# Second stage of a cross-attention and mixture block: logits of the slot pass stored in DRAM and turned on TensorE for the combine

## The reference

```python
x = x + _L1_ffn_ref(_layernorm(x, axis=-1), L1_ffn_phi, L1_ffn_W, L1_ffn_b)
...
logits = jnp.einsum('bmd,dnp->bmnp', x, phi)
dispatch = jax.nn.softmax(logits, axis=0)
...
combine = jax.nn.softmax(logits.reshape(bsz, m, n * p), axis=-1).reshape(bsz, m, n, p)
slots = jnp.einsum('bmd,bmnp->bnpd', x, dispatch)
y = jnp.einsum('bnpd,nde->bnpe', slots, W) + b[None, :, None, :]
out = jnp.einsum('bnpd,bmnp->bmd', y, combine)
```

## Time and profile before

| what | us |
|---|---|
| median of 3 runs | 6867.51 |
| lowest and highest | 6865.7, 6872.63 |
| the profiled execution | 6864.03 |
| its span | 6862.2 |
| slot pass, first logits to first combine matmul | 4671.4 to 5906.9 |
| combine, first to last matmul | 5906.9 to 6856.7 |

### The profile page before, as it was taken

The page is one execution under the profiler, slowest core; times in us unless marked ns, Lnnn a source line. Parts: engine busy times, 40 slices in busy tenths (PEclk is TensorE's granted clock), DMA queues, the critical chain, the costliest instruction groups (busy, mean ns, idle before and its releaser), DMA issues. The chain is left out here.

```text
span 6862.2 us, 93027 instructions
## 1 busy us (share of the span) xinstructions
PE 6307.0 (92%) x35933; PEld 3091.1 (45%) x35933; DVE 3514.3 (51%) x6804; ACT 3263.7 (48%) x6001; POOL 2408.1 (35%) x2689
## 2 busy tenths in 40 slices
PE   3799999999999999999999999966999999999999
PEld 1223333333333333333333333226888888666666
DVE  3565665665656656656656566516666666000000
ACT  1366666666666666666666666522222222111111
POOL 4226436346355264363463552342222222000000
PEclk9799999999999999999999999968999999999999
DMA  2442332432432423314324324003444444311110
GB/s 64 77 76 57 67 76 56 73 69 63 76 71 55 84 57 66 78 55 73 69 63 76 70 53 75 6 16 135 157 167 154 158 162 163 121 56 56 49 56 31
DMA packets 364938, 546.09 MB, mean 80 GB/s; under 512 B 59824, under 2 KB 281984, under 8 KB 364240
## 3 DMA queue, kind: packets, MB, share of 16 engines
q1 hardware_dynamic: 321232, 498.18, 30.0%
q10 hardware_dynamic: 43264, 41.95, 1.8%
HBM read 387.94 MB, written 151.28 MB: 79 GB/s over the span
## 5 line engine op out<-in xcount | busy, mean ns | idle before, releaser
L1193 DVE TENSOR_REDUCE mx<-psum 128x1 f32<-128x401 f32 x4096 | 2212.9, 570 | 1615.7 <-PE psum L767 1606.6
L1038 ACT ACTIVATE probs<-psum 128x512 f32<-128x512 f32 (+1 forms) x3328 | 1910.6, 599 | 910.4 <-PE psum L789 907.3
L767 PE MATMUL psum<-kst,qst 96*128 96x401 bf16 x4096 | 1356.6, 343 | 192.5 <-DVE mx L1193 149.6
L789 PE MATMUL psum<-qst,kst 99*128 99x512 bf16 (+1 forms) x3328 | 1286.0, 387 | 49.9 <-ACT probs L1038 44.8
L800 PE MATMUL psum<-probs,vaug 128*17 128x512 f32 x6656 | 886.8, 605 | 0.0
L789 PEld LDWEIGHTS psum<-qst,kst 99*128 99x128 bf16 (+1 forms) x3328 | 328.8, 99 | 1178.5 <-ACT probs L1038 748.9
L767 PEld LDWEIGHTS psum<-kst,qst 96*128 96x128 bf16 x4096 | 402.7, 98 | 962.8 <-DVE mx L1193 756.3
L1460 POOL TENSOR_TENSOR disp<-disp,rz 128x2048 f32<-128x2048 f32 x64 | 294.7, 4605 | 905.5 <-DVE rz L1679 905.5
L1479 PE MATMUL psum<-phi,xT 128*128 128x128 f32 x4096 | 511.0, 279 | 39.1 <-DMA xT<-xnT_scratch 31.8
L1630 ACT ACTIVATE disp<-psum 128x512 f32<-128x512 f32 x256 | 152.8, 597 | 807.6 <-PE psum L1547 807.6
L1479 PEld LDWEIGHTS psum<-phi,xT 128*128 128x128 f32 x4096 | 479.0, 193 | 86.8 <-issue 79.1
(11 more groups left out here) (197 smaller groups left out, 7556.2 us busy)
## 6 DMA issues: line engine op xcount, KB each, us to landing
xnb<-xn_scratch SPq DMA_DIRECT2D x256, 512.0 KB, 3.6
kst<-k_planes SPq DMA_DIRECT2D x384, 200.1 KB, 8.8
k_planes<-pl SPq DMA_DIRECT2D x96, 384.0 KB, 3.2
y_scratch<-ysb ACTq DMA_DIRECT2D x128, 256.0 KB, 3.3
disp<-y_scratch SPq DMA_DIRECT2D x16, 2048.0 KB, 9.2
vaug<-v_scratch SPq DMA_DIRECT2D x64, 442.0 KB, 4.6
v_scratch<-vst SPq DMA_DIRECT2D x48, 544.0 KB, 3.1
cin<-in_ctx SPq DMA_DIRECT2D x48, 512.0 KB, 3.8
```

The lines of the kernel that those rows point to most:

```text
L767: mm(to[:, 0:PW], qst[g][0:NP, j, t * P:(t + 1) * P], kst[g][0:NP, j, k0:k0 + PW], start=True, stop=True).then_inc(m_full, 1)
L789: mm(bank[S_BANK[n % 2]][0:m, :], kst[g][0:NR, j, c * P:c * P + m], qst[g][0:NR, j, :], start=True, stop=True).then_inc(s_full, 1)
L1038: fn(probs[0:m, 4 * (k % 2) + j, :], bank[S_BANK[j % 2]][0:m, :], ACT.Exp, scale=float(HD) ** 0.5).then_inc(s_exp, 1)
L1193: v.tensor_reduce(mx[:, n % 2, u // 4, u % 4:u % 4 + 1], bank[M_BANK[r % 2]][:, 0:PW], AX.X, ALU.max).then_inc(m_free, 1)
```

## The change

The combine no longer computes logits. In the slot pass ScalarE's queue stores every tile as soon as it is evacuated (`store_logits`, 1 MB in pieces of 512 bytes, to `logit_scratch`), and VectorE's `front` waits for that store before it overwrites the tile. For the combine SyncE reads a quarter of a batch's logits at a time (`logits_back`, a unit of 1 MB, tokens on partitions), eight units deep, into the memory of `xT`. ScalarE takes the exponentials in place, with the token's maximum as bias and the row sum as a second result (`weights`). TensorE turns four 128x128 blocks into a bank (`transpose_back`), VectorE copies the bank into `exT` (`copy_back`), and `combine` multiplies with 256 columns. The denominators come from the row sums. `ya` and the residuals take the memory of `phi`, `disp` and `xnb`.

```diff
...
+    lg_d = nc.dram_tensor("logit_scratch", (B, QT, P, NS), F32, kind="Internal").ap()
...
+        lgb = xT[:, :, :, :].rearrange("p b k s -> p (b k s)").rearrange("p (u t n) -> p u t n", u=8, t=QT)
...
+        ya = [phi[:, :, :].rearrange("p k n -> p (k n)").rearrange("p (c e) -> p c e", e=D),
+              flat[:, 0:NSL * D].rearrange("p (c e) -> p c e", e=D)]
+        x3 = [xnb[:, i, :, :] for i in range(2)]
+        exT = [flat[:, NSL * D + i * S:NSL * D + (i + 1) * S] for i in range(4)]
...
+
+            def logits_back(u):
+                if u >= 8:
+                    sp.wait_ge(tr_mm, 4 * (u - 7))
+                sp.dma_start(lgb[:, u % 8, :, :], lg_d[u // 4][:, :, QS * (u % 4):QS * (u % 4) + QS].rearrange(
+                    "t p n -> p t n")).then_inc(lg_in[u % 8], 16)
+
+            def values(b, c0, c1):
+                sp.dma_start(ya[b % 2][:, c0:c1, :],
+                             y_d[b].rearrange("(p c) e -> p c e", c=NSL)[:, c0:c1, :]).then_inc(y_in[b % 2], 16)
+
+            def residual(b):
+                sp.dma_start(x3[b % 2], x3_d[b].rearrange("(p t) d -> p t d", t=QT)).then_inc(x3_in[b % 2], 16)
...
+                    if s == NSL - 1 and b == 4:
+                        sp.wait_ge(l_mm, 4 * TILES)
+                        for i in range(2):
+                            sp.wait_ge(lg_stored[i], 16 * (TILES // 2))
+                        logits_back(0)
+                        logits_back(1)
+                    if s == NSL - 1 and b == 10:
+                        for i in range(2):
+                            sp.wait_ge(y_stored[i], 16 * PAIRS * (NSL - 1) // 2)
+                        values(0, 0, NSL - 1)
+
+            for u in range(2, 8):
+                logits_back(u)
+            sp.wait_ge(sl_mm, B * NSL)
+            for i in range(2):
+                residual(i)
...
+            values(0, NSL - 1, NSL)
+            values(1, 0, NSL)
+            for b in range(2, B + 2):
+                for h in range(4):
+                    if 4 * b + h < UNITS:
+                        logits_back(4 * b + h)
+                if b < B:
                     sp.wait_ge(o_mm, NSL * (b - 1))
-                values(b, 0, NSL)
-                if b >= 2:
+                    values(b, 0, NSL)
                     sp.wait_ge(o_stored[b % 2], 16 * (b // 2))
-                residual(b)
+                    residual(b)
...
+            def transpose_back(n):
+                b, e = n // NSL, n % NSL
+                u = 4 * b + e // 4
+                if e % 4 == 0:
+                    pe.wait_ge(c_exp, QT * (u + 1))
+                if n >= 4:
+                    pe.wait_ge(ex_ready, n - 3)
                 for t in range(QT):
-                    last = nc.tensor.transpose(tb[0:3, t * P:(t + 1) * P], ngp[:, t, b, :], identb[:, :])
-                last.then_inc(ng_tr, 1)
-
-            def scores(b, c):
-                n = b * NSL + c
-                if n >= 2:
-                    pe.wait_ge(c_exp, n - 1)
-                o = bank[n % 2]
-                for k in range(2):
-                    mm(o, phi[:, k, c * P:(c + 1) * P], xT[:, b, k, :], start=(k == 0), stop=False)
-                if c == 0:
-                    pe.wait_ge(shift_ready, b + 1)
-                mm(o, ones3[:, :], shift[b % 2], start=False, stop=True).then_inc(c_mm, 1)
-
-            def combine(b, e):
-                n = b * NSL + e
+                    last = nc.tensor.transpose(bank[n % 4][:, t * P:(t + 1) * P],
+                                               lgb[:, u % 8, t, (e % 4) * P:(e % 4 + 1) * P], ident[:, :])
+                last.then_inc(tr_mm, 1)
+
+            def combine(n):
+                b, e = n // NSL, n % NSL
+                pe.wait_ge(ex_ready, n + 1)
                 if e == 0:
-                    pe.wait_ge(y_in[b % 2], 16 * (b // 2 + 1))
-                    if b >= 1:
-                        pe.wait_ge(o_ready, b)
-                pe.wait_ge(c_exp, n + 1)
+                    pe.wait_ge(y_in[b % 2], 16 * (b // 2 + 1 + (b + 1) % 2))
                 for t in range(QT):
-                    last = mm(bank[4 + t][:, 0:D + 1], ex[n % 4][:, t * P:(t + 1) * P], ya[b % 2][:, e, :],
+                    if e == 0 and b >= 1:
+                        pe.wait_ge(o_ready, QT * (b - 1) + t + 1)
+                    last = mm(bank[4 + t][:, 0:D], exT[n % 4][:, t * P:(t + 1) * P], ya[b % 2][:, e, :],
                               start=(e == 0), stop=(e == NSL - 1))
                 last.then_inc(o_mm, 1)
...
+            def store_logits(n):
+                act.wait_ge(l_copied, 4 * n + 4)
+                if n >= 2:
+                    act.wait_ge(lg_stored[n % 2], 16 * (n // 2))
+                act.dma_start(lg_d[:, n % QT, :, (n // QT) * SL:(n // QT + 1) * SL].rearrange("b p n -> p b n"),
+                              disp[:, n % RING, :, :]).then_inc(lg_stored[n % 2], 16)
...
+            def weights(u):
+                b, h = u // 4, u % 4
+                act.wait_ge(lg_in[u % 8], 16 * (u // 8 + 1))
+                if u == 0:
+                    act.wait_ge(nm_ready, 1)
+                if h == 0 and b >= 2:
+                    act.wait_ge(o_den, b - 1)
+                for t in range(QT):
+                    d = lgb[:, u % 8, t, :]
+                    fn(d, d, ACT.Exp, bias=nm[:, t, b:b + 1], accum_out=sums[:, b % 2, t, h:h + 1]).then_inc(c_exp, 1)
...
+                store_logits(n)
...
+                if g == NSL * PAIRS - 2:
+                    weights(0)
...
+                    if g % 2 == 1:
+                        store_logits(n)
...
+            def store_out(b):
+                act.wait_ge(o_ready, QT * (b + 1))
+                act.dma_start(out[b].rearrange("(t p) d -> p t d", p=P), x3[b % 2]).then_inc(o_stored[b % 2], 16)
...
+            for u in range(1, 8):
+                weights(u)
+            for b in range(B):
+                for h in range(4):
+                    if 4 * b + h + 8 < UNITS:
+                        weights(4 * b + h + 8)
+                store_out(b)
...
+                dve.wait_ge(lg_stored[n % 2], 16 * (n // 2 + 1))
...
+                    if n == TILES:
+                        dve.wait_ge(ng_step, TILES)
+                        v.tensor_scalar(nm[:, :, :], negs[:, :, :], -1.0, None, ALU.mult).then_inc(nm_ready, 1)
...
+            def copy_back(n):
+                dve.wait_ge(tr_mm, n + 1)
+                if n >= 4:
+                    dve.wait_ge(o_mm, n - 3)
+                v.tensor_copy(exT[n % 4], bank[n % 4]).then_inc(ex_ready, 1)
+
+            def denominators(b):
+                dve.wait_ge(c_exp, QT * 4 * (b + 1))
+                v.tensor_reduce(den[:, :], sums[:, b % 2, :, :], AX.X, ALU.add).then_inc(o_den, 1)
+                dve.wait_ge(o_den, b + 1)
+                v.reciprocal(rc[:, b % 2, :], den[:, :]).then_inc(o_rc, 1)
+                dve.wait_ge(o_rc, b + 1)
...
             def finish(b):
                 dve.wait_ge(o_mm, NSL * (b + 1))
-                for t in range(QT):
-                    ins = v.reciprocal(rc[:, b % 2, t:t + 1], bank[4 + t][:, D:D + 1])
-                ins.then_inc(o_rc, 1)
-                dve.wait_ge(o_rc, b + 1)
                 dve.wait_ge(x3_in[b % 2], 16 * (b // 2 + 1))
                 for t in range(QT):
-                    ins = v.scalar_tensor_tensor(out=x3[b % 2][:, t, :], in0=bank[4 + t][:, 0:D],
-                                                 scalar=rc[:, b % 2, t:t + 1], in1=x3[b % 2][:, t, :],
-                                                 op0=ALU.mult, op1=ALU.add)
-                ins.then_inc(o_ready, 1)
-
-            shift_rows(0)
-            for b in range(B):
-                if b + 1 < B:
-                    shift_rows(b + 1)
-                finish(b)
+                    v.scalar_tensor_tensor(out=x3[b % 2][:, t, :], in0=bank[4 + t][:, 0:D],
+                                           scalar=rc[:, b % 2, t:t + 1], in1=x3[b % 2][:, t, :],
+                                           op0=ALU.mult, op1=ALU.add).then_inc(o_ready, 1)
...
```

More of the change, by code:

```diff
@@ L1386, in stage_two @@
         ng_step = sem("ng_step")
[L1387 to L1391, removed]
+        nm_ready = sem("nm_ready2")
+        lg_stored = [sem(f"lg_stored{i}") for i in range(2)]
+        lg_in = [sem(f"lg_in{i}") for i in range(8)]
         y_in = [sem(f"y_in{i}") for i in range(2)]
         x3_in = [sem(f"x3_in{i}") for i in range(2)]
-        c_mm = sem("c_mm")
         c_exp = sem("c_exp")
+        tr_mm = sem("tr_mm")
+        ex_ready = sem("ex_ready")
         o_mm = sem("o_mm")
+        o_den = sem("o_den")
         o_rc = sem("o_rc")
@@ L1561, in _ @@
             pe.wait_ge(y_ready, PAIRS * NSL)
[L1562 removed]
+            pe.wait_ge(l_copied, 4 * TILES)
             for n in range(B * NSL + LAG):
[L1564 removed]
                 if n < B * NSL:
[L1566 to L1568 removed]
+                    transpose_back(n)
                 if n >= LAG:
[L1570 removed]
```

(50 more changed lines are left out.)

43 lines of the change are left out of this document (5 added, 38 removed).

## The result

The changed kernel takes **6932.92 us**, the median of five runs (6910.85 to 6939.99), against 6867.51 us (6864.94 to 6872.63, five runs): a ratio of 1.0086, with a 95% interval of 1.0067 to 1.0106. It is slower by 65 us, where 6492 us were forecast. The gain that was forecast and the loss that hides it can both be read from its profile. The profiled execution took 6918.06 us, with a span of 6916.3.

What follows compares the result with a forecast made beforehand. TensorE was taken to bound the slot pass and the combine. The terms -378 - 2 - 8 + 2 + 3 + 6 + 2 = -375 us gave 6489 profiled, 6492 us as median, range 6465 to 6610.

Steps and rivals of the forecast that it cites:

- the likeliest case: Whole kernel: the forecast of 6492 us, given 0.73, with its own range of 6465 to 6530 us.
- The combine tile: Combine: four transposes replace recomputed logits, a tile takes 2.18 us instead of 3.67; 378 us less, plus 2 and 8.
- the rival of doubled ones: Combine: transposes run as full float32 products in two recorded instructions each, 113 us more, 6605 us; chance 0.04.
- What keeps pace in the combine: Combine: VectorE's copy 0.67 us, ScalarE's exponential 0.60, both under 2.18 a tile; transfers need 211 GB/s; nothing counted.
- The store's landing: Slot pass: each 1 MB store in 2048 pieces lands in 6.5 us, with 4.9 and 9.2 as bounds.
- 13.0 us of cover: Slot pass: a landing of up to 6.7 + 6.3 = 13.0 us costs TensorE nothing in steady state.
- the stores also share the DMA engines with the token loads: Slot pass: stores add 1.05 MB to a tile's 2.9 MB; 3 us added, between 0 and 15.
- The rivals of the slow store: Slot pass: landing beyond 13.0 us delays VectorE, middle 6587 us (0.13); from 19.2 us the whole gain goes (0.03).
- The sign of being wrong: Slot pass: steps longer than 9.2 us with VectorE waiting for a DMA of `logit_scratch` would point to the store.
- The first tile: Start of slot pass: VectorE's subtraction waits for the first store, 2 us; 0 if landing in 4.9, 4.3 at 9.2.
- The end of the slot pass: Last slice to first combine product: combine loads queued ahead delay token loads; 6 us later, from 4 earlier to 22 later.
- The clock: End of slot pass: longer TensorE idling may add a second piece at the lower clock level, 2 us.

Runs made afterwards that it cites:

- The kernel with 512 bytes of padding: The changed kernel with the batches of the stored logits 4 MiB + 512 bytes apart instead of 4 MiB: 6507.49 us, ratio 0.9471.
- The kernels with late loads: Combine's first loads moved behind the last token load, against the same layouts with early loads: 8 KB layout 6484.07 us, 512 bytes of padding 6487.32 us.

## Why the prediction was wrong

The kernel with 512 bytes of padding is the changed kernel without the fault. Its median of 6507.5 us is 15 us above the forecast, inside the likeliest case's own range, so its profiled execution (6506.09 us, span 6504.3) serves to measure each term.

- **The combine tile, right.** Forecast -378 - 2 - 8 = -388 us; measured from the first product to the end -386.8 in the changed kernel and 6504.3 - 5936.70 - 955.3 = -387.7 in the padded one. The transposes took one record each, as L823 does; the rival of doubled ones is out:

```profile
L1556 PE MATMUL psum<-ident,xT x1024: 272/273/478, 6335.4 to 6905.7; 128*128 128x128 f32 x171
```

- **What keeps pace in the combine, right.** TensorE is busy for 496.75 of 500 us, with VectorE's copy at 0.69 us, as taken from the earlier trace rows, and 191 GB/s. ScalarE's exponential takes 0.71 and not 0.60, and a second instruction that reads the row sums out takes 0.19; that was not in the prediction, and at 0.9 against 2.16 us it costs nothing:

```profile
L1613 ACT ACTIVATE xT<-xT,nm x256: 704/707/725, 6321.3 to 6842.9; 128x512 f32<-128x512 f32 x128
L1613 ACT ACTIVATION_READ_ACCUMULATOR xT<-xT,nm x256: 183/186/192, 6321.9 to 6843.5; 128x1 f32 x128
```

- **The store's landing, the step that failed.** "I take 6.5, near the row of the same bytes" took the size of a piece and the bytes from rows whose pieces lie close together. With the batches a little off 4 MiB it was a good estimate (5.7). At exactly 4 MiB it was 14.9, 70 GB/s, outside both ends. The first store took 12.5 us already (issued at 4680.65, VectorE's subtraction at 4693.15), and only the second store, issued at 4687.79, ran beside it; so other traffic explains only a small part. The prediction named the rule of the Trainium skill that speaks against these addresses (DMA: Bandwidth & Descriptors, Latency and other measured facts), and took its figure as 10.2 us, which on the prediction's own path costs 5 us; so the rule alone would have moved the forecast by those 5 us. The runs bear the rule out at 4 MiB, more strongly than its 103 GB/s, and its remedy too: 4 KiB more restore the speed (5.8 us). They differ at 2 MiB, where that page of the Trainium skill has a loss (164 GB/s, for copies in rows of 16 KiB) and this store has none.
- **What the landing costs, the larger part of the failure.** Even with 14.9 us the prediction's own working gives 6492 + 58 x 1.9 + 8 = 6610 us. Measured are 6933. It priced a slow store only through VectorE, which waits for it, with 13.0 us of cover. That wait was idle time, as the kernel without it shows. The price is the 3 us of the sentence "the stores also share the DMA engines with the token loads": the term counted the store's bytes, 1.05 MB beside 2.9, and not the time for which its packets hold the engines. That term was 403 us, 267 of waiting for token loads and 136 of lower clock. It also took the slack too large, a load of 3.6 us against a step of 9.2: each of the two buffers of `xnb` is loaded once a step, and it is free only outside its own products. Before, the load issued at 5104.46 was needed at 5111.68, 7.2 us later, and one of the 256 took longer than that. In the changed kernel 120 did; the one above took 11.4 and TensorE waited 4.18. For a store at full speed the term would have been right within its bounds: 5.9 us for the 116 steps in the padded kernel.
- **The rivals of the slow store** (0.13, and 0.03 for the whole gain) had the slow store right, but the path and with it the price wrong: both go through VectorE's wait and its 13.0 us of cover. They put the point of no gain at 19.2 us; it was passed at 14.9. The sign of being wrong that the prediction named, long steps with VectorE waiting for `logit_scratch`, was there too, and pointed at that same path: it shows that the store is slow, not that VectorE's wait is what costs.
- **The first tile, right in the padded kernel:** the first step came 2.8 us later than before, forecast 2. In the changed kernel it was 8.
- **The end of the slot pass, too small.** Forecast 6 us for tail and first product; measured in the padded kernel 16.3 (last 12 copies) + 4.8 (from there to the first product) = 21.1. The term that failed is the tail, 6.5 with 11.7 as its upper bound: two steps that stand behind the 2.1 MB of logits and the 1.9 MB of values took 13.5 and 11.7 us against 6.0 and 5.9 before, 13.3 us more, so nothing of either transfer was hidden. The kernels with late loads show that this is the cause: 20 of the 21 us came back.
- **The clock**, 2 us, was taken for the end of the pass and can't be told from the rest there. In the slot pass, where nothing was taken, it cost 136 us in the changed kernel and nothing in the padded one (a granted clock of 1.00 in both stretches).

So the sum for a store that behaves comes to -387.7 + 2.8 + 5.9 + 21.1 = -357.9 us, which is 6506.09 - 6864.03; the forecast for it was -375.

## What to carry to other kernels

Price a new transfer twice: by when it lands, for those who wait for it, and by how long its packets hold the DMA engines, for all others who use them; look at the addresses that are under way together, and where no row of the profile has their like and a rule warns of them, put in the cheap padding first. An idle time of 505 us beside one of 296 says nothing on which of them matters: follow the engine that bounds the kernel, and ask what it waits for. A load for the next stage, placed ahead of loads that the present stage is short of, cost its full length here.

## What the runs showed of the hardware

512-byte writes that go round over 16 rows exactly 4 MiB apart land at 70 GB/s (1 MB in 14.9 us). 512 bytes more between the rows are enough for 5.7 us, and rows 1 or 2 MiB apart are as good (5.6 and 5.7 us). The loss is in what is under way together: four rows at a time to the same addresses lose 81 us in the first 116 steps and sixteen lose 403. What in the memory makes it so, no run tells. The damage is mostly to others: packets of another queue that are not slower themselves come late on the shared engines, 11.3 us in place of 3.9 for a token load. And the gaps that this leaves on TensorE cost twice: after one of 4.18 us, 32 products took 6.26 us in place of 3.74, at a granted clock of 0.59; over the slot pass, at a granted clock of 0.90, this made a third of the loss (136 of 403 us).
